# Decoder layer, attention stage: the split of the projected queries moves from ScalarE and VectorE (out of PSUM) to GpSimd (out of an SBUF copy), and the weight blocks stand in other pairs

## The chip, the cores and the metric

The kernel runs on one core of one Trainium2 chip. The metric is the device time of one execution, in microseconds (us). TensorE is called PE in the profile, VectorE DVE, ScalarE ACT, GpSimd POOL and SyncE SP; SP issues nearly all of the DMAs.

## The reference, cut to what matters

One decoder layer on four sequences of 512 tokens with 1024 features, in float32: a state-space mixer, then cross-attention over 1601 keys per sequence, then a feed-forward layer with 4-bit weights (3584 inner features), each followed by a residual add and a layer norm. The change is in the cross-attention, 16 heads with a latent of 64:

```python
C_q = Q @ Wq_d                                   # (b, n, 128)
C_kv = K @ Wkv_d                                 # (b, nkv, 64)
CqWqk = (C_q @ W_qk).reshape(b, n, H, LKV)       # the projection: queries of each head
scores = jnp.einsum('bnhl,bkl->bhnk', CqWqk, C_kv) / sqrt(LKV)
attn = softmax(scores)
out = jnp.einsum('bhnk,bkhd->bnhd', attn, (C_kv @ Wv_u).reshape(b, nkv, H, HD))
```

The weights of the feed-forward layer come as integers with integer zeros; `weight - zero` is formed for 84 blocks of 128 x 1024 while the attention runs.

## The kernel before, in words

Three stages run one after the other: the mixer (to about 318 us), the attention (to about 1426 us) and the feed-forward layer (to the end).

The attention handles four batches (sequences) of 16 heads, that is 64 heads; a head has four units of 128 queries, so there are 256 units (`NU`), numbered u or k, and 64 units to a batch. Two units make a pair (`PAIRS` = 128, 32 to a batch), numbered p. Heads are projected two at a time, so every eight units form one cycle with one projection.

Every engine walks the same loop over k, in an order written out by hand. In step k, PE computes the second half of the scores of unit k (L1019), then a projection (L999), an output product (L1057) or a turn of latent keys where one is due, then half of a weighting product (`weigh`, L1038), the transposes of the last three key tiles of unit k-1 (`turn`, L1048), and the first half of the scores of unit k+1. DVE takes the maximum of the second half of unit k (`maximum`, L1190), then what is due, then transposes the probabilities of unit k-1 in blocks (`turn`, L1197) into `tn`, then the maximum of the first half of unit k+1 (`first_maximum`, L1179). ACT computes the exponents of both halves (`exponent`, L1101), and PE may write the second half of the scores of unit k+1 only after the exponent of the second half of unit k has left that bank. ACT also copies the turned tiles (`keep_turned`, L1108), the weighted latents (`out_latent`, L1122) and, after each odd step, two of the blocks of a pair (`cross`, L1116).

The transposed blocks of a pair must change partitions before PE can weigh with them: SP moves nine of 16 blocks by DMA (`exchange`, L912), POOL copies five (`blocks`, L1315) and ACT two. Three buffers `pt` take them. The transposed tiles `tn` have two buffers, so DVE's transposes of pair p+2 wait until all blocks of pair p have moved (`moved`).

POOL's order in pair p: the five block copies; in odd pairs the sums of the denominators (L1322) and the residual add of a head (L1330); then, if the pair has a weight block, `prepare` (L1357 subtracts the zeros, L1359 casts); then steps of the layer norm of the batch before (`root_step` in pairs 17 to 19 of a batch, `factors` and `normalise`, L1334, in pairs 20 to 23); in pair 2 of two batches `split_keys` (L1305, L1307). SP's order in pair p: the store of the block of pair p-1, which waits for POOL's cast (L926); the exchange; the load of the next block; rows of the layer norm in pairs 23 to 30. `FREE` names the 11 of 32 pairs of a batch without a weight block; 84 blocks stand in the other pairs.

A score is computed with queries and keys each split in a high part (rounded to fp32r) and a low part (the rest). High and low parts of a query share the 128 partitions of `qs`: for the first head of a projection the high part stands in partitions 0 to 63 and the low part in 64 to 127, for the second head the other way round. Before the change, ACT writes the two high parts from the projection's PSUM bank `mi` (L1087, L1088), and DVE subtracts them from the same bank (L1172, L1174). This is done at steps k with k % 8 = 5, for the heads whose scores begin three units later. The bank `mi` is shared in a fixed order by projections, transposes, outputs and latent turns; after a projection the next one waits for DVE's second subtraction (`bank_free`, L897).

Of the kernel before, what the change touches and what calls it, by code (L numbers as in the profile page):

```python
# [11 lines left out]
P = 128  # L12
# [14 lines left out]
LAT = 64  # L27
# [760 lines left out]
PER_BATCH = len(BLOCKS) // L  # L788
FREE = (2, 5, 8, 11, 14, 20, 21, 22, 23, 30, 31)
LATE = 3 * (PAIRS // L)  # L790
# [32 lines left out]
def attention(nc, d, kvd, cq, ident, shared, raw, wint, x1, x2):  # L823

    with ExitStack() as ctx:
# [11 lines left out]
        s_cnp, s_cn = sem("cn_ps"), sem("cn")  # L837
        s_q, s_qh, s_ql = sem("q"), sem("qh"), sem("ql")
        s_sc, s_nm, s_ex, s_tt = (sem(n) for n in ("scores", "nm", "ex", "turned"))
# [9 lines left out]
        keys = keys_of(shared)  # L849
        wqk, wv, cn, kv = (keys[n] for n in ("wqk", "wv", "cn", "kv"))  # L850
        y0 = sb("b_y0", [P, QT, HID])
        rw = [sb(f"b_rw{j}", [P, HID], I32) for j in range(2)]
# [8 lines left out]
        pt.append(shared[:, NXC + 2 * NSZ - 8 * SEG:NXC + 2 * NSZ].rearrange("p (a z e) -> p a z e", a=4, z=2))  # L861
        pe = [sb(f"b_pe{j}", [P, NKT - NDT, 2, P]) for j in range(3)]
        ot = sb("b_ot", [P, NB])
        yo = sb("b_yo", [P, 2, QT, LAT])
# [28 lines left out]
        def bank_free(eng, ev):  # L893
            if AT[ev]:
                kind, g, e = EVENTS[AT[ev] - 1]
                if kind == "project":
                    eng.wait_ge(s_ql, g + 2)  # L897
                elif kind == "turn":
                    eng.wait_ge(s_pe, g + 1)
                elif kind == "cn":  # L900
                    eng.wait_ge(s_cn, 2 * (g - 1) + e + 1)
                else:
                    eng.wait_ge(s_yo, g + 1)
# [177 lines left out]
        def scalar():  # L1081
# [3 lines left out]
            def project(g):  # L1085
                S.wait_ge(s_q, g // 2 + 1)
                S.copy(qs[g // 2 % 2][0:LAT, 0, :], mi[0:LAT, :]).then_inc(s_qh, 1)  # L1087
                S.copy(qs[g // 2 % 2][LAT:P, 1, :], mi[LAT:P, :]).then_inc(s_qh, 1)  # L1088

# [62 lines left out]
        def vector():  # L1152
# [15 lines left out]

            def project(g):
                q = qs[g // 2 % 2]  # L1170
                V.wait_ge(s_qh, g + 1)
                V.tensor_tensor(q[LAT:P, 0, :], mi[0:LAT, :], q[0:LAT, 0, :].bitcast(F32), ALU.subtract).then_inc(s_ql, 1)  # L1172
                V.wait_ge(s_qh, g + 2)
                V.tensor_tensor(q[0:LAT, 1, :], mi[LAT:P, :], q[LAT:P, 1, :].bitcast(F32), ALU.subtract).then_inc(s_ql, 1)  # L1174
# [88 lines left out]
            low_keys(0)  # L1263
            project(0)
            low_keys(1)
# [4 lines left out]
            for k in range(NU + OUT_AT):  # L1270
                if k < NU:
                    maximum(k)
                if k % 8 == 5 and k + 3 < NU:
                    project((k + 3) // 4)
                if k % 4 == OUT_AT % 4 and k >= OUT_AT:
                    output((k - OUT_AT) // 4)
                if k in CN_AT:
                    keep_latent(*CN_AT[k])
                if 1 <= k <= NU:
                    turn(k - 1)  # L1280
                if k + 1 < NU:
                    first_maximum(k + 1)
                if k < NU:
                    norm_piece(k)
# [15 lines left out]
        def gpsimd():  # L1300
# [8 lines left out]
            def blocks(p):  # L1309
# [4 lines left out]
                for n, (a, c) in enumerate(BY_POOL):  # L1314
                    G.tensor_copy(pt[p % MOVES][32 * c:32 * c + 32, a, :, :], tn[s][32 * a:32 * a + 32, c, :, :]).then_inc(s_block, 1)  # L1315
                    G.wait_ge(s_block, len(BY_POOL) * p + n + 1)

            def sums(g):
# [44 lines left out]
            for p in range(PAIRS + 4):  # L1363
# [15 lines left out]
                if n == 2 and 1 <= b <= 2:  # L1379
                    split_keys(b + 1)  # L1380

        late, last_stores = sync()
# [582 lines left out]
```

## Time and profile before

| what | before |
|---|---|
| median of 3 runs | 2738.9 us (2735.4 to 2747.54) |
| the profiled execution | 2740.16 us, its span 2738.2 us |
| granted PE clock | 0.988 of full speed |
| busy over the span | PE 95%, DVE 85%, POOL 72%, ACT 61% |
| busy from 600 to 700 us (attention) | PE 96.60, DVE 92.52, POOL 79.25, ACT 77.03 us of 100 |

The span is the time from the first to the last instruction, and 2.0 us of the profiled execution lie around it. A matmul's end is modelled and overlaps the next matmul, so a busy PE says little; what counts is the distance from one score product to the next. "Idle before" tells how long an engine sat idle ahead of an instruction and which engine released it.

### The profile page before, as it was taken

What the parts mean: (1) busy time and instruction counts of PE and PEld (TensorE: products, weight loads), DVE (VectorE), ACT (ScalarE), POOL (GpSimd) and SP (SyncE); (2) the same over time, 40 slices, a digit from 0 to 9 for tenths busy, and PEclk for the clock granted to TensorE, in tenths of its full rate; (3) what the DMA queues carried; (4) which work ended last, traced back from release to release, by engine and by line L of the source; (5) the groups of instructions that cost most, each with busy time, mean ns of one, the idle gap of its engine ahead of it and who ended that gap; (6) DMA issues with size and microseconds to landing.
All of it is one profiled execution on the core that took longest, in us unless ns stands there. A gap on an engine that the chain in (4) does not pass through costs nothing.

```text
span 2738.2 us, 42011 instructions
## 1 busy us (share of the span) xinstructions
PE 2602.3 (95%) x14328; PEld 1979.5 (72%) x14328; DVE 2315.4 (85%) x2664; ACT 1670.2 (61%) x2619; POOL 1966.1 (72%) x1473
## 2 busy tenths in 40 slices
PE   7998899999999999999988999999999999999997
PEld 4665666666666666666656888888888888788885
DVE  2766688989998999899857999899998899899988
ACT  3444687877787778787855445454455555555553
POOL 1002377677777778777857999999887888888883
PEclk9899999999999999999999999999999999999999
DMA  7426677687778776877681222112223222132221
GB/s 276 157 100 206 212 236 216 188 240 206 223 214 261 206 219 204 259 228 221 201 278 69 100 93 93 70 70 70 77 70 123 77 85 78 70 116 79 83 93 77
DMA packets 166792, 420.64 MB, mean 154 GB/s; under 512 B 30130, under 2 KB 57652, under 8 KB 166068
## 3 DMA queue, kind: packets, MB, share of 16 engines
q1 hardware_dynamic: 164276, 409.57, 47.2%
q10 hardware_dynamic: 2304, 8.39, 0.8%
q8 instruction: 115, 1.88, 0.3%
q14 instruction: 97, 0.79, 0.1%
HBM read 248.43 MB, written 75.04 MB: 118 GB/s over the span
## 4 chain that ended last, share of the span: by engine, by line
PE 44%; SPq 3%; DVE 2%; POOL 1%; issue 1%; ACT 1%; DMA 1%; POOLq 0%; ACTq 0%; DVEq 0%
PE c_ps L1610 42%; SPq L912 2%; PE c_ps L1622 1%; DVE c_sum_g L1766 0%; DVE c_stats L1826 0%; DMA c_ident<-in_ident 0%; POOL b_rw L1357 0%; PE c_ps L1631 0%; POOL c_sum_g L1851 0%; PE b_po L1038 0%; PE b_sc L1019 0%; DVE c_acc L1766 0%; DMA b_rz<-in_c_dz 0%; DMA b_rz<-in_c_gz 0%; ACT c_sg L1674 0%
## 5 line engine op out<-in xcount | busy, mean ns | idle before, releaser
L1766 DVE SCALAR_TENSOR_TENSOR c_acc<-c_ps,c_sd,c_acc 128x1024 f32<-128x1024 f32 x440 | 562.9, 1282 | 90.8 <-PE c_ps L1610 90.7
L1668 ACT ACTIVATE c_scaled<-c_ps,c_sgu 128x1024 f32<-128x1024 f32 x336 | 375.2, 1117 | 422.5 <-PE c_ps L1610 414.7
L1101 ACT ACTIVATE b_pr<-b_sc,b_nm 128x799 f32<-128x799 f32 (+1 forms) x512 | 477.7, 935 | 169.4 <-DVE b_pr L1190 146.9
L1851 POOL TENSOR_TENSOR c_sum_u<-c_sum_u,c_scaled 128x1024 f32<-128x1024 f32 x168 | 404.8, 2410 | 99.6 <-ACT c_scaled L1668 98.3
L1851 POOL TENSOR_TENSOR c_sum_g<-c_sum_g,c_scaled 128x1024 f32<-128x1024 f32 x168 | 405.1, 2411 | 73.2 <-ACT c_scaled L1668 72.2
L1019 PE MATMUL b_sc<-b_kh,b_qs 128*128 128x402 f32 (+1 forms) x1024 | 398.6, 389 | 45.0 <-ACT b_pr L1101 41.2
L1197 DVE STREAM_TRANSPOSE b_tn<-b_pr 128x1280 f32<-128x1280 f32 x256 | 385.4, 1506 | 28.7 <-ACT b_pr L1101 14.6
L1315 POOL COPY b_pt<-b_tn 32x640 f32<-32x640 f32 x430 | 307.4, 715 | 141.7 <-DVE b_tn L1197 82.5
L1019 PE MATMUL b_sc<-b_kl,b_qs 128*128 128x402 f32 (+1 forms) x1024 | 355.9, 348 | 0.0
L1766 DVE SCALAR_TENSOR_TENSOR c_sum_g<-c_ps,c_sgu,c_sum_g 128x1024 f32<-128x1024 f32 x224 | 286.4, 1278 | 26.0 <-PE c_ps L1610 20.6
L1190 DVE TENSOR_SCALAR_CACHE_REDUCE b_pr<-b_sc,b_nm_first 128x799 f32<-128x799 f32 x256 | 268.7, 1050 | 29.1 <-PE b_sc L1019 8.3
L1766 DVE SCALAR_TENSOR_TENSOR c_sum_u<-c_ps,c_sgu,c_sum_u 128x1024 f32<-128x1024 f32 x224 | 285.7, 1276 | 6.5 <-POOL c_sum_u L1851 4.4
L1610 PE MATMUL c_ps<-c_hh,c_dw_int 128*128 128x512 f32 x896 | 277.9, 391 | 11.3 <-POOL c_hl L1867 7.1
L1179 DVE TENSOR_REDUCE b_nm_first<-b_sc 128x1 f32<-128x802 f32 x256 | 250.8, 980 | 44.8 <-PE b_sc L1019 40.3
L1610 PE MATMUL c_ps<-c_xh,c_gw_int 128*128 128x512 f32 x896 | 279.6, 393 | 5.3 <-DVE c_sum_u L1766 3.8
L1610 PE MATMUL c_ps<-c_xh,c_uw_int 128*128 128x512 f32 x896 | 278.6, 392 | 3.4 <-DVE c_xl L1771 2.3
L1019 PEld LDWEIGHTS b_sc<-b_kh,b_qs 128*128 128x128 f32 x1024 | 193.6, 189 | 119.0 <-ACT b_pr L1101 77.0
L1610 PE MATMUL c_ps<-c_xl,c_gw_int 128*128 128x512 f32 x896 | 277.0, 390 | 0.0
L1610 PE MATMUL c_ps<-c_hl,c_dw_int 128*128 128x512 f32 x896 | 276.6, 390 | 0.0
L1610 PE MATMUL c_ps<-c_xl,c_uw_int 128*128 128x512 f32 x896 | 276.5, 390 | 0.0
L1038 PE MATMUL b_po<-b_pt,shared 128*64 128x256 f32 x1720 | 258.9, 389 | 3.4 <-DMA b_pt<-b_tn 2.6
L764 POOL TENSOR_TENSOR a_xt<-a_xt,a_bup 128x1024 f32<-128x1024 f32 x16 | 37.6, 2355 | 264.6 <-DMA a_xt<-in_a_x 207.5
(212 smaller groups left out, 4871.0 us busy)
## 6 DMA issues: line engine op xcount, KB each, us to landing
b_pt<-b_tn SPq DMA_DIRECT2D x774, 80.0 KB, 2.7
shared<-b_tn SPq DMA_DIRECT2D x378, 80.0 KB, 2.8
c_uw_int<-wint_u SPq DMA_DIRECT2D x56, 512.0 KB, 3.5
c_gw_int<-wint_g SPq DMA_DIRECT2D x56, 512.0 KB, 3.4
c_dw_int<-wint_d SPq DMA_DIRECT2D x56, 512.0 KB, 3.4
a_cx<-in_b_ctxT SPq DMA_DIRECT2D x16, 1608.0 KB, 9.8
b_rw<-in_c_gw SPq DMA_DIRECT2D x28, 512.0 KB, 4.1
b_rz<-in_c_gz SPq DMA_DIRECT2D x28, 512.0 KB, 5.6
```

Source lines behind the costliest of these rows:

```text
L912: Q.dma_start(pt[p % MOVES][32 * c:32 * c + 32, a, :, :].rearrange("p t e -> p (t e)"), tn[s][32 * a:32 * a + 32, c, :, :].rearrange("p t ...
L1019: ins = T.matmul(sc[:, at:at + n], qs[g // 2 % 2][:, g % 2, q * P:(q + 1) * P], k[b % 2][:, k0:k0 + n], start=(z == 0), stop=(z == 1))
L1038: ins = T.matmul(po[z * LAT:(z + 1) * LAT, s * 256:(s + 1) * 256], cn[:, b, t, :], turned, start=(t < 2), stop=(t >= NKT - 2))
L1101: S.activation(pr[u % 2][:, k0:k1], sc[:, at + lo:at + hi], ACT.Exp, bias=nm[:, u % 2:u % 2 + 1], accum_out=den[:, g % 2, q, half:half + 1 ...
L1179: V.tensor_reduce(nm0[:, u % 2:u % 2 + 1], sc[:, at + SIDE[0][0]:at + SIDE[0][1]], AX, ALU.max, negate=True).then_inc(s_part, 1)
L1190: V.tensor_scalar(pr[u % 2][:, SIDE[1][2]:SIDE[1][3]], sc[:, at + SIDE[1][0]:at + SIDE[1][1]], -1.0, nm0[:, j], ALU.mult, ALU.min, accum_o ...
L1197: V.transpose(tn[u // 2 % 2][:, :, u % 2, :], pr[u % 2][:, 0:4 * SEG].rearrange("p (c e) -> p c e", c=4)).then_inc(s_tt, 1)
L1315: G.tensor_copy(pt[p % MOVES][32 * c:32 * c + 32, a, :, :], tn[s][32 * a:32 * a + 32, c, :, :]).then_inc(s_block, 1)
L1610: ins = T.matmul(pair[slot % 4][:, b * 512:(b + 1) * 512], w[n][t % 2][:, k * P:(k + 1) * P], v[:, b * 512:(b + 1) * 512], start=(z == 0), ...
L1668: S.activation(dst[:, :], pair[SLOT[x, t] % 4][:, :], ACT.Identity, scale=scale(x, t)).then_inc(s_e, 1)
L1766: V.scalar_tensor_tensor(out=total, in0=pair[SLOT[x, t] % 4][:, :], scalar=scale(x, t), in1=before, op0=ALU.mult, op1=ALU.add).then_inc(s_ ...
L1851: G.tensor_tensor(total, total, scaled[m % 2][:, :], ALU.add).then_inc(s_add, 1)
```

## The change

ACT now copies the whole projection bank (128 x 512) to a new SBUF tile `qf` in one instruction, and the bank is free after that copy. POOL makes the high parts and the low parts from `qf` in four instructions, at the end of its pairs p with p % 4 = 1; 31 projections go this way. The first projection (g = 0) keeps the old way. The pairs without a weight block become 1, 2, 5, 9, 13, 17, 21, 23, 25, 29 and 31 of each batch instead of 2, 5, 8, 11, 14, 20, 21, 22, 23, 30 and 31; their number stays at 11.

```diff
-FREE = (2, 5, 8, 11, 14, 20, 21, 22, 23, 30, 31)
+FREE = (1, 2, 5, 9, 13, 17, 21, 23, 25, 29, 31)
...
+        qf = shared[:, keys_end:keys_end + NB]
...
                 if kind == "project":
-                    eng.wait_ge(s_ql, g + 2)
+                    eng.wait_ge(s_qf, g // 2) if g else eng.wait_ge(s_ql, 2)
...
             def project(g):
                 S.wait_ge(s_q, g // 2 + 1)
-                S.copy(qs[g // 2 % 2][0:LAT, 0, :], mi[0:LAT, :]).then_inc(s_qh, 1)
-                S.copy(qs[g // 2 % 2][LAT:P, 1, :], mi[LAT:P, :]).then_inc(s_qh, 1)
+                if g == 0:
+                    S.copy(qs[0][0:LAT, 0, :], mi[0:LAT, :]).then_inc(s_qh, 1)
+                    S.copy(qs[0][LAT:P, 1, :], mi[LAT:P, :]).then_inc(s_qh, 1)
+                else:
+                    S.wait_ge(s_ql, g)
+                    S.copy(qf, mi[:, :]).then_inc(s_qf, 1)
...
-            def project(g):
-                q = qs[g // 2 % 2]
-                V.wait_ge(s_qh, g + 1)
+            def project_first():
+                q = qs[0]
+                V.wait_ge(s_qh, 1)
...
             for k in range(NU + OUT_AT):
                 if k < NU:
                     maximum(k)
-                if k % 8 == 5 and k + 3 < NU:
-                    project((k + 3) // 4)
...
+            def split_queries(g):
+                q = qs[g // 2 % 2]
+                G.wait_ge(s_qf, g // 2)
+                for z, (high, low) in enumerate(((slice(0, LAT), slice(LAT, P)), (slice(LAT, P), slice(0, LAT)))):
+                    G.tensor_copy(q[high, z, :], qf[high, :]).then_inc(s_qh, 1)
+                    G.wait_ge(s_qh, g + z + 1)
+                    G.tensor_tensor(q[low, z, :], qf[high, :], q[high, z, :].bitcast(F32), ALU.subtract).then_inc(s_ql, 1)
+                    G.wait_ge(s_ql, g + z + 1)
...
                 if n == 2 and 1 <= b <= 2:
                     split_keys(b + 1)
+                if p % 4 == 1 and 2 * p + 6 < NU:
+                    split_queries((p + 3) // 2)
```

## Rows read from the trace of the kernel before

**Rows 1.** PE timeline, score products: start us, us long, [idle before, releaser].

```profile
351.77 0.45 PE L1019 MATMUL b_sc<-b_kh,b_qs 128*128 128x402 f32 x1 [1.07 <-ACT b_pr L1101]
...
779.49 0.35 PE L1019 MATMUL b_sc<-b_kh,b_qs 128*128 128x402 f32 x1
...
783.73 0.43 PE L1019 MATMUL b_sc<-b_kh,b_qs 128*128 128x402 f32 x1
...
788.24 0.45 PE L1019 MATMUL b_sc<-b_kh,b_qs 128*128 128x402 f32 x1 [0.45 <-ACT b_pr L1101]
...
791.45 0.45 PE L1019 MATMUL b_sc<-b_kh,b_qs 128*128 128x402 f32 x1
...
792.54 0.43 PE L1019 MATMUL b_sc<-b_kh,b_qs 128*128 128x402 f32 x1
...
796.45 0.35 PE L1019 MATMUL b_sc<-b_kh,b_qs 128*128 128x402 f32 x1
...
1368.81 0.45 PE L1019 MATMUL b_sc<-b_kh,b_qs 128*128 128x402 f32 x1 [0.44 <-ACT b_pr L1101]
```

**Rows 2.** DVE timeline of the same cycle.

```profile
777.62 1.51 DVE L1197 STREAM_TRANSPOSE b_tn<-b_pr 128x1280 f32<-128x1280 f32 x1
...
780.79 1.05 DVE L1190 TENSOR_SCALAR_CACHE_REDUCE b_pr<-b_sc,b_nm_first 128x799 f32<-128x799 f32 x1
...
781.91 0.69 DVE L1172 TENSOR_TENSOR b_qs<-b_mi,b_qs 64x512 fp32r<-64x512 f32 x1
782.62 0.69 DVE L1174 TENSOR_TENSOR b_qs<-b_mi,b_qs 64x512 fp32r<-64x512 f32 x1
...
785.99 1.05 DVE L1190 TENSOR_SCALAR_CACHE_REDUCE b_pr<-b_sc,b_nm_first 128x799 f32<-128x799 f32 x1
```

**Rows 3.** ACT timeline of the same cycle.

```profile
781.29 0.58 ACT L1087 CAST b_qs<-b_mi 64x512 fp32r<-64x512 f32 x1 [0.94 <-PE b_mi L999]
...
785.31 1.47 ACT L1116 COPY shared<-b_tn 32x640 f32<-32x640 f32 x2
787.17 0.93 ACT L1101 ACTIVATE b_pr<-b_sc,b_nm 128x799 f32<-128x799 f32 x1 [0.39 <-PE b_mi L1048]
```

**Rows 4.** Who waited for whom, whole span: us in total, times, longest.

```profile
PE b_sc L1019 <- ACT b_pr L1101: 41.2, 83, 1.8
...
PE b_po L1038 <- DMA shared<-b_tn: 3.5, 3, 2.5
...
DVE b_tn L1197 <- DMA b_pt<-b_tn: 6.4, 4, 2.3
DVE b_tn L1197 <- DMA shared<-b_tn: 5.7, 3, 3.4
...
SPq L927 <- POOL b_rw L1359: 41.1, 41, 3.0
```

**Rows 5.** Groups by line, 480 to 1400 us: busy us, mean ns | idle before.

```profile
L1122 ACT COPY b_ot<-b_po 128x512 f32<-128x512 f32 x55 | 31.7, 576 | 0.0
...
L1334 POOL TENSOR_SCALAR b_y<-b_y,b_rstd,b_nmr 128x1024 f32<-128x1024 f32 x12 | 14.5, 1205 | 0.6
...
L1307 POOL TENSOR_TENSOR b_kl<-shared,b_kh 128x1601 fp32r<-128x1601 f32 x2 | 7.3, 3635 | 0.2
...
L1305 POOL CAST b_kh<-shared 128x1601 fp32r<-128x1601 f32 x2 | 3.0, 1521 | 0.1
```

**Rows 6.** POOL timeline of an odd pair with a weight block.

```profile
812.22 3.82 POOL L1315 COPY b_pt<-b_tn 32x640 f32<-32x640 f32 x5 [1.07 <-DVE b_tn L1197]
...
816.97 2.37 POOL L1357 TENSOR_TENSOR b_rw<-b_rw,b_rz 128x1024 int32<-128x1024 int32 x1
819.40 1.04 POOL L1359 CAST b_rw<-b_rw 128x1024 fp32r<-128x1024 int32 x1
```

**Rows 7.** Durations of one line: ns min/median/max, first and last start us.

```profile
L1315 POOL COPY b_pt<-b_tn x430: 707/714/726, 335.4 to 1415.1; 32x640 f32<-32x640 f32 x144
```

**Rows 8.** Page, part 1: each engine's busy us (share of the span) xinstructions.

```profile
PE 2602.3 (95%) x14328; PEld 1979.5 (72%) x14328; DVE 2315.4 (85%) x2664; ACT 1670.2 (61%) x2619; POOL 1966.1 (72%) x1473
```

More of the change, by code:

```diff
@@ L837, in attention @@
         s_cnp, s_cn = sem("cn_ps"), sem("cn")
-        s_q, s_qh, s_ql = sem("q"), sem("qh"), sem("ql")
+        s_q, s_qh, s_ql, s_qf = sem("q"), sem("qh"), sem("ql"), sem("q_kept")
         s_sc, s_nm, s_ex, s_tt = (sem(n) for n in ("scores", "nm", "ex", "turned"))
@@ L850, in attention @@
         wqk, wv, cn, kv = (keys[n] for n in ("wqk", "wv", "cn", "kv"))
+        keys_end = KPAD + 2 * HEADS * LAT + L * NKT * LAT
         y0 = sb("b_y0", [P, QT, HID])
@@ L1167, in keep_latent @@
                               mi[:, 0:len(chunk) * LAT].rearrange("p (t e) -> p t e", e=LAT)).then_inc(s_cn, 1)
-            def project(g):
-                q = qs[g // 2 % 2]
-                V.wait_ge(s_qh, g + 1)
+            def project_first():
+                q = qs[0]
+                V.wait_ge(s_qh, 1)
                 V.tensor_tensor(q[LAT:P, 0, :], mi[0:LAT, :], q[0:LAT, 0, :].bitcast(F32), ALU.subtract).then_inc(s_ql, 1)
-                V.wait_ge(s_qh, g + 2)
+                V.wait_ge(s_qh, 2)
                 V.tensor_tensor(q[0:LAT, 1, :], mi[LAT:P, :], q[LAT:P, 1, :].bitcast(F32), ALU.subtract).then_inc(s_ql, 1)
@@ L1263, in vector @@
             low_keys(0)
-            project(0)
+            project_first()
             low_keys(1)
```

## Prediction

> **What bounds the kernel now.** I read the PE timeline first, as starts of the second-half score product (L1019), one per unit. The rows at 779.49, 783.73, 788.24, 792.54 and 796.45 [rows 1] are units 109 to 113; 109 % 8 = 5, so the projection falls in the first step. The steps last 4.24, 4.51, 4.30 and 3.91 us. The reader is to see that three of the four carry no idle time: PE runs from product to product. Only the third start (788.24) waited, for ACT's exponent. The second and the fourth step hold the same PE work (scores, the first part of a weighting product, three transposes): 3.91 without a wait, 4.51 with it. So the stall costs 0.60 us. It is more than the 0.45 shown as idle, since the rows let one matmul's modelled end overlap the next. This start stands in each of the 31 cycles with a projection inside the loop, the first at 351.77 and the last at 1368.81, with 0.44 us of idle or more. Between these two lie 240 units, 30 cycles: 1017.04 / 30 = 33.90 us a cycle, 8.48 a pair.
>
> Then the DVE timeline of the same cycle [rows 2]. The maximum of unit 109 ends about 781.85; two subtractions follow from 781.91 to 783.31; only then comes the transpose and the next first-half maximum, and the maximum of unit 110 starts at 785.99. Its scores began at 783.73; for unit 109 the maximum began 780.79 - 779.49 = 1.30 after them, here 2.26. DVE is late by about 1 us because of the 1.4 us of subtractions. Last, ACT [rows 3]: it waits 0.94 for the projection, spends 1.2 on two copies, runs through a block copy from 785.31 to 786.78, and starts the exponent that PE waits for at 787.17, after 0.39 of waiting. The view names PE as the releaser there, but what came in just then is DVE's maximum (785.99 + 1.05 + 0.08 of read-out). So the split of the queries sets PE's stall, by way of DVE.
>
> The view of waits shows the rest [rows 4]: 41.2 us of PE idle for exponents in 83 waits, of which the 31 above are the largest regular part. Most of the others stand two steps ahead of the next projection, behind ACT's other block copies, and stay. DMA of moved blocks costs DVE 12.1 us in 7 waits and PE 3.5 in 3, near the ends of batches. SP waits for POOL's cast 41 times.
>
> **The change, part by part.** *DVE* loses 2 x 0.69 plus gaps, 1.4 us, 31 times [rows 2]. The transpose moves up to 781.9, and the first-half maximum of unit 110 is then ready when its scores are (they end a little before 783.73); the maximum of unit 110 can start about 1.1 to 1.3 after 783.73, at 785.0, not 785.99. *ACT* swaps two copies of 0.58 for one; the nearest row is its copy of a whole bank, 128x512 in 0.576 [rows 5], so it gains 0.6 us, and its block copy ends near 786.2. The exponent then starts at 786.2 to 786.3 and frees the bank near 787.2, while PE is ready only at 783.73 + 3.91 = 787.64. PE's own work covers all of it with 0.4 to spare: 31 x 0.60 = **18.6 us gained**. ACT's new wait on the split of the projection before is eight units old and costs nothing. The bank is released at 781.87 instead of 783.31; PE's transposes want it at about 783.5, so little is gained there. Steps where layer-norm statistics also sit on DVE start with DVE less late; I add 3 us for them (some ten steps at about 0.3), between bounds of 0 and 10 (the rest of the 41.2 that isn't ACT's).
>
> *POOL* gains four instructions, 31 times. The cast of 128x1601 took 1521 ns and the subtraction 3635 [rows 5], that is 0.95 and 2.27 ns an element; for 512 elements 0.49 and 1.16. Shorter instructions cost more an element: a block copy takes 714 ns for 640 [rows 7], 1.12 each, so 0.57 for 512, and by the same addition 1.25 for the subtraction. With a wait for its own result behind each, a split takes 2 x 1.82 and some gaps, 3.7 to 4.0; I take 3.9, in all 121 us on an engine that is busy for 1966.1 [rows 8]. Only half of the partitions are used; the block copies use 32 and take no less an element, so I expect no saving. No row has a subtraction that writes other partitions than it reads; block copies that do lie in the same 707 to 726 ns, so I take none as the extra, and keep 7 us a split as the far end.
>
> What hides it: an odd pair with a block takes from 812.22 to 820.44, 8.2 us [rows 6]; an even one lacks sums and residual add (816.04 to 816.97), 7.3; an odd pair without a block and with a split 4.75 + 3.9 = 8.65. The new order gives, in four pairs, 7.3 + 8.65 + 7.3 + 8.2 = 31.45 against a cycle of 33.3 (33.9 less 0.6). POOL fits, with 1.85 us to spare. The split's deadline: the transpose that releases the pair ends at 779.13 [rows 2], the scores that need the first head start at 791.45 [rows 1]: 12.3 us, 11.7 after the gain. POOL needs 4.75 for the pair's own work and 1.95 for the first head: 6.7. It may be 5 us late before PE waits.
>
> It is late once in each batch but the first. Pairs 17 to 22 now hold splits in 17 and 21, blocks in 18, 19, 20 and 22, and a root step or a normalise (1.2 us, [rows 5]; the root steps I cost alike) in each: 8.65 + 7.3 + 8.2 + 7.3 + 8.65 + 7.3 + 6 x 1.2 = 54.6 against 6 x 8.3 = 49.8. POOL ends 4.8 us late, where pairs 20 to 23 were free of blocks before. Late next is SP: it issues the store of a pair's block ahead of the next exchange, and the nine block moves, the next load and the norm's rows queue behind that wait. The cast of pair 22 comes 4.8 + 7.3 = 12.1 after its transposes, so exchange 23 starts some 4 us late. In the trace such waits reached 3.0 us and 41.1 in all, with only 7 DVE waits on moves [rows 4], so I charge 1.5 us in three batches: **4.5 lost**, between 0 and 5 us a batch.
>
> *The weight blocks.* Before, runs of five and six pairs with blocks stood one after the other in each batch (15 to 19, 24 to 29); now none is longer than three. The 15.6 us of waits for moved blocks [rows 4] came behind the long runs near batch ends. I let 9 of them go, between 0 and 15.6.
>
> **Sum.** 18.6 + 3 + 9 - 4.5 = 26 us off the profiled execution's 2740.2 (span 2738.2 and 2.0 around it): 2714. The profiled execution is 1.3 us above the median of 2738.9; the forecast stays at **2714**, 0.9% below the median.
>
> **Rivals.** (a) *POOL and SP eat the gain.* The lateness in pairs 17 to 23 isn't absorbed: about 5 us a batch in three batches, and the waits at batch ends stay: 18.6 + 3 - 15 = 7 off, 2733. For it: POOL's load rises by 121 us and the store wait couples it to SP. Against: POOL is idle again by pair 31.
>
> (b) *Slower: the split takes longer.* The place is POOL in pairs 1, 5, 9 and so on. From 3.9 + 1.85 = 5.75 us a split on, POOL sets the cycle; beyond 6.4 the cycle exceeds 33.9; at 7 it is 34.55, 0.65 x 31 = 20 us slower: 2760. For it: the shifted, two-input form has no row.
>
> (e) *Slower: the splits block DVE.* Before, DVE gave 1.4 us a cycle; held off for the 3.9 of a split it would lose 2.5 x 31 = 78 us: up to 2818; it decides from 1.4 us of blocking a split on. The block copies keep to 707 to 726 ns beside a DVE that is busy for nine tenths [rows 7], so nothing that the two do now blocks. The Trainium skill, Perfetto Trace Analysis, Optimizing Scalar/DVE Operations, warns that VectorE and GpSimd share an SBUF read port, so that moving work between them might not help; by that rule (e) would come true, and the trace doesn't agree so far.
>
> (c) *All moved-block waits go and the layer-norm pairs cost nothing*: 18.6 + 3 + 15.6 = 37 off, 2703.
>
> (d) *PE's stall stays*, because ACT's block copy alone holds back the exponent. Then only 9 - 4.5 = 4.5 are left: 2736. Against: the 0.39 that ACT idled ahead of that exponent [rows 3], and the 0.6 it gains.
>
> **Chances and range.** Forecast 0.55 (its own range 2706 to 2722), (a) 0.15, (b) 0.07, (e) 0.03, (c) 0.12, (d) 0.08. The measurement tells about 0.5%, 14 us. Forecast and (c) are faster, and a third of (a): 0.72; the rest of (a) and (d), within 0.5%: 0.18; (b) and (e), slower: 0.10. The range takes in (a), (c) and (d) with their bounds and leaves out (b) and (e): 2698 to 2741.
>
> **What the new profile would show.** Right: no start of a score product behind k % 8 = 6 waits for ACT, the second step is 3.9 instead of 4.5, the cycle near 33.2; ACT's bank copy takes 0.58; POOL's cast and subtraction on 64x512 take 0.5 to 0.6 and 1.15 to 1.3. Waits of DVE for moved blocks shrink near pairs 28 to 31 and appear at 23 to 25. The forecast is wrong if PE waits for POOL's split, if DVE's transposes or POOL's copies get longer, or if the exponent of step 6 stays as late as before.

## The result, and the profile after

The changed kernel takes 2727.1 us in the median of 5 runs (2725.0 to 2727.4), against 2738.9: ratio 0.9948, 95% interval 0.9932 to 0.9963. The profiled execution takes 2725.14 us with a span of 2721.3, that is 15.0 us less than before, where the sum of the prediction said 26 less (2714). The range (2698 to 2741) and the sign hold; the sum is 11 us too good, and the forecast's own range (2706 to 2722) is missed by 5. Lines have moved: scores L1019 is L1021, DVE's maximum L1190 is L1196, its transposes L1197 are L1203, ACT's exponent L1101 is L1107, the weighting product L1038 is L1040, SP's moves L912 and store L927 are L914 and L929, GpSimd's subtraction and cast of a weight block L1357 and L1359 are L1370 and L1372; new are ACT's bank copy L1094 and the split, L1326 and L1328.

The PE timeline of the kernel after: second-half score products of units 13, 101 to 105, and 253, which answer to [rows 1].

```profile
373.62 0.35 PE L1021 MATMUL b_sc<-b_kh,b_qs 128*128 128x402 f32 x1
...
736.32 0.35 PE L1021 MATMUL b_sc<-b_kh,b_qs 128*128 128x402 f32 x1
...
740.55 0.43 PE L1021 MATMUL b_sc<-b_kh,b_qs 128*128 128x402 f32 x1
...
744.46 0.35 PE L1021 MATMUL b_sc<-b_kh,b_qs 128*128 128x402 f32 x1
...
748.67 0.43 PE L1021 MATMUL b_sc<-b_kh,b_qs 128*128 128x402 f32 x1
...
752.58 0.35 PE L1021 MATMUL b_sc<-b_kh,b_qs 128*128 128x402 f32 x1
...
1379.39 0.35 PE L1021 MATMUL b_sc<-b_kh,b_qs 128*128 128x402 f32 x1
```

The steps from 736.32 are 4.23, 3.91, 4.21 and 3.91, and no start waits. Before they were 4.24, 4.51, 4.30 and 3.91. The undisturbed cycle of eight units fell from 33.03 to 32.33 us: 0.60 at the stalled step, as forecast, and 0.1 at the next.

DVE's timeline of this cycle, which answers to [rows 2], and below it ACT's, which answers to [rows 3].

```profile
737.61 1.05 DVE L1196 TENSOR_SCALAR_CACHE_REDUCE b_pr<-b_sc,b_nm_first 128x799 f32<-128x799 f32 x1
...
738.59 1.51 DVE L1203 STREAM_TRANSPOSE b_tn<-b_pr 128x1280 f32<-128x1280 f32 x1
740.50 0.99 DVE L1185 TENSOR_REDUCE b_nm_first<-b_sc 128x1 f32<-128x802 f32 x1 [0.40 <-PE b_sc L1021]
741.60 1.05 DVE L1196 TENSOR_SCALAR_CACHE_REDUCE b_pr<-b_sc,b_nm_first 128x799 f32<-128x799 f32 x1
```

```profile
738.12 0.59 ACT L1094 COPY shared<-b_mi 128x512 f32<-128x512 f32 x1 [0.94 <-PE b_mi L1001]
...
741.60 1.47 ACT L1122 COPY b_pt<-b_tn 32x640 f32<-32x640 f32 x2
743.09 0.93 ACT L1107 ACTIVATE b_pr<-b_sc,b_nm 128x799 f32<-128x799 f32 x1
```

The transpose follows the maximum at once, and the next maximum starts 1.05 us behind its scores (741.60 against 740.55) where it was 2.26. The exponent at 743.09 starts straight behind ACT's block copy: DVE's maximum was in at 742.65, so ACT is now the last in that step, with little to spare.

GpSimd's lines and ACT's copy after: ns min/median/max, first and last start (the block copies answer to [rows 7]).

```profile
L1326 POOL CAST b_qs<-shared x62: 599/607/613, 345.9 to 1352.9; 64x512 fp32r<-64x512 f32 x62
```

```profile
L1328 POOL TENSOR_TENSOR b_qs<-shared,b_qs x62: 1257/1277/1292, 346.5 to 1353.6; 64x512 fp32r<-64x512 f32 x62
```

```profile
L1319 POOL COPY b_pt<-b_tn x430: 706/713/723, 334.5 to 1399.0; 32x640 f32<-32x640 f32 x144
```

```profile
L1094 ACT COPY shared<-b_mi x31: 585/586/587, 343.4 to 1348.5; 128x512 f32<-128x512 f32 x31
```

So far all is as costed: 0.61 and 1.28 where 0.57 and 1.25 were taken, a split lasts 4.0 us with its gaps, for 3.9, and block copies are as long as before. The page, part 1, which answers to [rows 8], has GpSimd 112 us busier and DVE 41 us less:

```profile
PE 2598.3 (95%) x14328; PEld 1982.2 (73%) x14328; DVE 2274.3 (84%) x2602; ACT 1651.3 (61%) x2588; POOL 2078.3 (76%) x1597
```

The loss is in the waits. Waits of the whole span after, which answer to [rows 4]:

```profile
PE b_sc L1021 <- ACT b_pr L1107: 29.7, 59, 1.6
...
DVE b_tn L1203 <- DMA b_pt<-b_tn: 12.3, 10, 2.5
...
DVE b_tn L1203 <- DMA shared<-b_tn: 7.3, 5, 2.7
DVE b_tn L1203 <- issue: 7.2, 5, 4.1
...
PE b_po L1040 <- DMA shared<-b_tn: 5.0, 3, 2.3
```

SP's own waits, 340 to 1430 us:

```profile
SPq L929 <- POOL b_rw L1372: 53.6, 41, 4.5
```

PE waits 29.7 us for exponents, not 41.2. But the three rows of waits for moved blocks that [rows 4] has (12.1 on DVE, 3.5 on PE) now sum to 24.6, not 15.6, and SP stands 53.6 us before GpSimd's casts, not 41.1. The row "issue" (0.5 us before) is more of the same: in each of its five cases a move had landed 0.08 us ahead of the transpose. The prediction let 9 of the 15.6 go.

The stretch from unit 13 to unit 253 (30 cycles) splits the result in two: 30 undisturbed cycles, and the rest, which is what late blocks, statistics and the like add.

| | 13 to 253 | 30 undisturbed cycles | rest |
|---|---|---|---|
| before | 1018.5 | 30 x 33.03 = 990.9 | 27.6 |
| after | 1005.8 | 30 x 32.33 = 969.9 | 35.9 |
| change | -12.7 | -21.0 | +8.3 |

The prediction had -18.6 in the first column of changes and -7.5 (3 and 9 off, 4.5 on) in the second. The first came out 2.4 better; the second missed by 15.8. (Of the span's 16.9 us, 1.6 are gained ahead of unit 13 and 2.6 behind unit 253.) How one such late step arises is seen in the longest, that of unit 112: it lasts from 781.42 to 789.43, 8.0 us, and 3.91 undisturbed. SP's timeline ahead of it:

```profile
769.46 0.58 SPq L921 DMA_DIRECT2D b_rw<-in_c_gw  x1
770.09 0.43 SPq L924 DMA_DIRECT2D b_rz<-in_c_gz  x1
770.62 1.12 SPq L947 DMA_DIRECT2D shared<-kvd  x2
771.78 0.58 SPq L929 DMA_DIRECT2D wint_d<-b_rw  x1
772.47 5.66 SPq L914 DMA_DIRECT2D shared<-b_tn  x9
```

GpSimd's, of the same time, and PE's:

```profile
771.24 1.21 POOL L1347 TENSOR_SCALAR b_y<-b_y,b_rstd,b_nmr 128x1024 f32<-128x1024 f32 x1
...
777.16 1.21 POOL L1347 TENSOR_SCALAR b_y<-b_y,b_rstd,b_nmr 128x1024 f32<-128x1024 f32 x1
778.31 0.61 POOL L1326 CAST b_qs<-shared 64x512 fp32r<-64x512 f32 x1
...
781.03 1.28 POOL L1328 TENSOR_TENSOR b_qs<-shared,b_qs 64x512 fp32r<-64x512 f32 x1
782.38 3.81 POOL L1319 COPY b_pt<-b_tn 32x640 f32<-32x640 f32 x5
```

```profile
784.65 2.38 PE L1040 MATMUL b_po<-shared 128*64 128x256 f32 x14 [2.25 <-DMA shared<-b_tn]
```

The nine moves are those of pair 21 of its batch. Pair 20 had no weight block before; now two loads of rows and the store of pair 20's block go out ahead of them, beside the next batch's keys, which stood there before, too. They were issued by 778.13, and PE gets what they bring at 784.65, 6.5 us later. GpSimd is late too: with two normalise steps and a split behind it, it begins the copies of pair 22 at 782.38, 6.0 us after that pair's last transpose (774.91 + 1.50). The new order alone is enough for such a step: in free_only, the kernel before with only that order (next section), the steps of units 112 and 113 are together 4.2 us longer than undisturbed ones.

The step cost PE more than its wait: PE sat idle for 2.25 us, and the step is 4.1 us too long. Most of the rest goes with TensorE's granted clock, seen in these two windows (us; busy us and instructions of PE, PEld, DVE, ACT and POOL; granted clock; DMA share; GB/s):

```profile
784.00:785.00 1.00, 0.34 (x4) 0.28 (x6) 0.31 (x1) 0.00 (x0) 0.94 (x2) 1.00 0.61 159
787.00:788.00 1.00, 1.00 (x5) 1.00 (x5) 0.89 (x2) 0.00 (x0) 1.00 (x1) 0.50 1.02 418
```

Behind the wait the granted clock is 0.50, that is 1.2 of 2.4 GHz, from 786 to 789 us, and score products last 0.54 us, for 0.35. Between 340 and 1390 us the trace of after has two such stretches (the other lies from 1346 to 1349), that of before has one.

### The profile page after: what moved, and what is told of

Read it like the earlier page. It is cut to its first block, busy times and chain, and to the rows that moved or that the text cites. A ratio compares the mean times of both kernels' runs of the same rounds, so it can differ in the third digit from the quotient of the medians.

```text
span 2721.3 us, 42088 instructions
## 1 busy us (share of the span) xinstructions
PE 2598.3 (95%) x14328; PEld 1982.2 (73%) x14328; DVE 2274.3 (84%) x2602; ACT 1651.3 (61%) x2588; POOL 2078.3 (76%) x1597
## 4 chain that ended last, share of the span: by engine, by line
PE 48%; POOL 5%; SPq 4%; ACT 2%; DVE 2%; issue 2%; DMA 1%; POOLq 0%; ACTq 0%; DVEq 0%
PE c_ps L1625 43%; SPq L914 3%; PE b_po L1040 2%; PE b_sc L1021 2%; POOL b_pt L1319 1%; POOL b_rw L1370 1%; PE c_ps L1637 1%; POOL shared L1319 1%; ACT b_pr L1107 1%; PE b_mi L1050 0%; POOL b_rw L1372 0%; DVE c_sum_g L1781 0%; POOL b_qs L1328 0%; DVE c_stats L1841 0%; POOL c_sum_g L1866 0%
## 5 line engine op out<-in xcount | busy, mean ns | idle before, releaser
L1107 ACT ACTIVATE b_pr<-b_sc,b_nm 128x799 f32<-128x799 f32 (+1 forms) x512 | 477.1, 933 | 176.5 <-DVE b_pr L1196 158.1
L1021 PE MATMUL b_sc<-b_kh,b_qs 128*128 128x402 f32 (+1 forms) x1024 | 397.1, 388 | 35.9 <-ACT b_pr L1107 29.7
L1203 DVE STREAM_TRANSPOSE b_tn<-b_pr 128x1280 f32<-128x1280 f32 x256 | 385.4, 1506 | 39.0 <-DMA b_pt<-b_tn 12.3
L1021 PE MATMUL b_sc<-b_kl,b_qs 128*128 128x402 f32 (+1 forms) x1024 | 356.1, 348 | 0.0
L1196 DVE TENSOR_SCALAR_CACHE_REDUCE b_pr<-b_sc,b_nm_first 128x799 f32<-128x799 f32 x256 | 268.6, 1049 | 30.0 <-PE b_sc L1021 9.4
L1021 PEld LDWEIGHTS b_sc<-b_kh,b_qs 128*128 128x128 f32 x1024 | 193.7, 189 | 103.2 <-ACT b_pr L1107 58.4
L1040 PE MATMUL b_po<-b_pt,shared 128*64 128x256 f32 x1720 | 258.9, 389 | 1.8 <-DMA b_pt<-b_tn 1.0
```

The source lines that it names most:

```text
L1021: ins = T.matmul(sc[:, at:at + n], qs[g // 2 % 2][:, g % 2, q * P:(q + 1) * P], k[b % 2][:, k0:k0 + n], start=(z == 0), stop=(z == 1))
L1040: ins = T.matmul(po[z * LAT:(z + 1) * LAT, s * 256:(s + 1) * 256], cn[:, b, t, :], turned, start=(t < 2), stop=(t >= NKT - 2))
L1107: S.activation(pr[u % 2][:, k0:k1], sc[:, at + lo:at + hi], ACT.Exp, bias=nm[:, u % 2:u % 2 + 1], accum_out=den[:, g % 2, q, half:half + 1 ...
L1196: V.tensor_scalar(pr[u % 2][:, SIDE[1][2]:SIDE[1][3]], sc[:, at + SIDE[1][0]:at + SIDE[1][1]], -1.0, nm0[:, j], ALU.mult, ALU.min, accum_o ...
L1203: V.transpose(tn[u // 2 % 2][:, :, u % 2, :], pr[u % 2][:, 0:4 * SEG].rearrange("p (c e) -> p c e", c=4)).then_inc(s_tt, 1)
```

## The experiments

Each line below is one kernel; "rest" is the distance from unit 13 to unit 253 less 30 of its own undisturbed cycles, from its profiled execution alone, and the two sums of waits are those of 340 to 1430 us (rows named "issue" left out). The experiments were timed beside runs of before with medians of 2741.6 to 2742.9, so the ratios compare better than the medians do. Executions of one kernel differ by up to 13 us (old_free: 2738.3 to 2751.4), and the profiled one of store_mid is 5.8 us below its median, so a difference of a few us in the rest says little where the ratios don't tell two kernels apart.

| kernel | median us | ratio to before, interval | cycle | rest | SP waits for casts | DVE and PE wait for moves and GpSimd's copies |
|---|---|---|---|---|---|---|
| before | 2738.9 | | 33.03 | 27.6 | 41.1 | 19.5 |
| after | 2727.1 | 0.9948, 0.9932 to 0.9963 | 32.33 | 35.9 | 53.6 | 31.0 |
| free_only | 2730.7 | 0.9968, 0.9956 to 0.9980 | 33.03 | 21.6 | 20.1 | 14.7 |
| old_free | 2743.8 | 1.0011, 0.9999 to 1.0023 | 32.33 | 51.3 | 69.8 | 37.1 |
| dve_filler | 2729.4 | 0.9961, 0.9949 to 0.9972 | 32.68 | 26.6 | 43.1 | 28.1 |
| act_two | 2728.6 | 0.9962, 0.9947 to 0.9976 | 32.68 | 32.1 | 59.1 | 32.2 |
| split_double | 2766.2 | 1.0092, 1.0075 to 1.0109 | 32.33 | 78.8 | 127.0 | 63.2 |
| norm_short | 2720.5 | 0.9931, 0.9914 to 0.9948 | 32.33 | 31.8 | 43.4 | 28.7 |
| order20 | 2724.4 | 0.9949, 0.9931 to 0.9968 | 32.33 | 35.6 | 52.3 | 27.0 |
| store_late | 2738.8 | 0.9992, 0.9982 to 1.0003 | 32.33 | 48.8 | none shown | 50.1 |
| prep_short | 2711.3 | 0.9878, 0.9863 to 0.9894 | 32.33 | 20.4 | 0.4 | 19.2 |
| rz_short | 2720.0 | 0.9914, 0.9900 to 0.9928 | 32.33 | 27.7 | 61.0 | 23.1 |
| prep_first | 2722.3 | 0.9929, 0.9917 to 0.9941 | 32.33 | 36.1 | 45.7 | 29.7 |
| store_mid | 2719.4 | 0.9908, 0.9893 to 0.9924 | 32.33 | 27.2 | 6.8 | 25.4 |

**The two parts alone.** free_only is the kernel before with only the new order of the weight blocks; old_free is the kernel after with the old order.

```diff
-FREE = (2, 5, 8, 11, 14, 20, 21, 22, 23, 30, 31)
+FREE = (1, 2, 5, 9, 13, 17, 21, 23, 25, 29, 31)
```

> The kernel before with only the new order of the weight blocks; the queries are split by ScalarE and VectorE as before. Theory (VectorE's subtractions make TensorE's stall, the order does not): the start of the score product behind k % 8 = 6 still waits 0.44 us or more in all 31 cycles, the cycle stays near 33.0, and the time lies within 10 us of 2739, since the order only moves the waits for moved blocks. Rival (the order of the blocks makes the gain): about 2727.

> The changed kernel with the old order of the weight blocks, so that GpSimd's splits fall on pairs that have a block too (1, 9, 13, 17, 25, 29 of a batch). Theory: plain cycles keep 3.91 us in the step k % 8 = 6, but such a pair costs GpSimd 8.2 + 3.9 = 12.1 us against a pair of 8.2, so it is 4 us late there, more in the long runs 15 to 19 and 24 to 29, TensorE waits for the split or the moved blocks, and the time is 5 to 40 us above 2727. Rival (the order is neutral, GpSimd has slack enough): 2727.

In free_only the stall is unchanged, as this start of its PE timeline shows, and the rest falls by 6.0. The time, 2730.7, lies in the theory's window, but at its edge: the order has a gain of its own.

```profile
749.48 0.46 PE L1019 MATMUL b_sc<-b_kh,b_qs 128*128 128x402 f32 x1 [0.45 <-ACT b_pr L1101]
```

In old_free the stall is gone and the cycle is 32.33, but the rest grows by 23.7 and eats all of it. Its waits:

```profile
DVE b_tn L1203 <- DMA b_pt<-b_tn: 19.8, 11, 2.5
...
DVE b_tn L1203 <- DMA shared<-b_tn: 10.7, 6, 3.0
...
PE b_sc L1021 <- POOL b_qs L1328: 8.5, 6, 2.1
```

So the order alone is worth 0.3%, the split alone nothing, and both together 0.5%. They don't add: the order pays for part of what the split costs GpSimd.

**What the stall was.** dve_filler puts a maximum over 1280 columns of an SBUF tile on DVE (1.48 us, its result unused) where the two subtractions stood.

```diff
+                if k % 8 == 5 and k + 3 < NU:
+                    V.tensor_reduce(idle[:, :], shared[:, KPAD:KPAD + 1280], AX, ALU.max)
```

> The changed kernel, with an unused maximum over 1280 columns (about 1.4 us) on VectorE where the two subtractions stood, 31 times; it reads SBUF and nothing waits for it. Theory: TensorE's stall at k % 8 = 6 comes back with 0.4 to 0.6 us in the 31 cycles, 14 to 19 us: 2741 to 2746. Rival (ScalarE's single copy or the early release of the bank removed the stall): 2727 to 2730.

DVE's timeline of dve_filler in the cycle of unit 101:

```profile
741.23 1.05 DVE L1197 TENSOR_SCALAR_CACHE_REDUCE b_pr<-b_sc,b_nm_first 128x799 f32<-128x799 f32 x1
...
742.20 1.48 DVE L1281 TENSOR_REDUCE b_idle<-shared 128x1 f32<-128x1280 f32 x1
...
746.09 1.05 DVE L1197 TENSOR_SCALAR_CACHE_REDUCE b_pr<-b_sc,b_nm_first 128x799 f32<-128x799 f32 x1
```

From maximum to maximum DVE needs 4.86 us here, 5.20 before (780.79 to 785.99, [rows 2]) and 3.99 after; the step is 4.18, 4.51 and 3.91. From 5.20 to 4.86 both fall by about a third of a microsecond. The filler holds DVE for less time than the subtractions did (the transpose behind it starts 2.37 us after the maximum, for 2.56), and it brings back only 0.27 of the 0.60. The exponent that PE waits for is late because of DVE here, as ACT's timeline shows:

```profile
747.26 0.93 ACT L1108 ACTIVATE b_pr<-b_sc,b_nm 128x799 f32<-128x799 f32 x1 [0.58 <-DVE b_pr L1197]
```

That DVE's lateness makes the stall stands; the size that was expected of the filler doesn't, and the time, 2729.4, lies in the rival's window. The new fact is in the total: 30 cycles are 0.35 longer, 10.5 us, and the kernel is slower by only 2 (by the ratios some 4, and their intervals overlap), because the rest shrinks by 9.3.

act_two copies the bank in two halves on ACT, 0.59 us more in a cycle.

```diff
-                    S.copy(qf, mi[:, :]).then_inc(s_qf, 1)
+                    for half in (slice(0, LAT), slice(LAT, P)):
+                        S.copy(qf[half, :], mi[half, :]).then_inc(s_qf, 1)
```

> The changed kernel with the bank copied in two halves of 64 partitions, so that ScalarE spends 1.2 us as before the change and the bank is released 0.6 us later. Theory: TensorE's own work covers it (0.4 us to spare in my working), the time rises by 0 to 6 us over 2727. Rival (ScalarE's saved 0.6 us is what removed the stall): the stall at k % 8 = 6 comes back, 2741 to 2746.

The step becomes 4.15, so of the 0.59 added 0.24 shows, and ACT had 0.35 to spare, for the 0.4 of the prediction. ACT's side, too, was thus worth part of the stall: with its two copies left, only 0.36 of the 0.60 would have gone. Here the rest falls by only 3.8 of the 10.5 us that 30 cycles are longer: the stretch from unit 13 to unit 253 is 6.7 us longer than after. The profiled time hides it (2727.1, for 2725.1), because this execution was 4.4 us shorter ahead of unit 13, and the ratio isn't told apart from that of the kernel after.

**How much GpSimd can take.** split_double does each subtraction of a split twice, which makes a split some 6.6 us, for 4.0.

```diff
+                    G.tensor_tensor(q[low, z, :], qf[high, :], q[high, z, :].bitcast(F32), ALU.subtract).then_inc(s_qh, 1)
+                    G.wait_ge(s_qh, 2 * (g + z))
```

> The kernel after, with each of the two subtractions of a split done twice on GpSimd: 2 x 1.28 us and two waits more, 2.6 to 2.8 us in each of 31 cycles. Theory (GpSimd has 32.3 - 31.5 = under 1 us of a cycle to spare, so from there on it sets the cycle): cycles grow by 1.7 to 2.2 us, 50 to 65 us in all, 2775 to 2795. Rival (GpSimd is late only in places and has the time elsewhere, as its share of busy time of 0.76 says): 2730 to 2745.

It is slower than after by 39.1 us, 1.26 in each of 31 cycles, for 2.6 to 2.7 more work: GpSimd had about 1.4 us of a cycle to spare, and neither figure expected fits. In the waits the excess stands where it was looked for: SP waits 127 us for casts, DVE and PE 63 for moves. The prediction's rival (b) would have come true with such a split, and more sharply than it said: it put the point from which the kernel is slower than before at 6.4 us a split, and one of 6.6 is 0.9% slower already, some 25 us.

**Where GpSimd's lateness comes from.** norm_short and order20 aim at pairs 17 to 25.

```diff
-                G.tensor_scalar(y[b % 2][:, q, :], y[b % 2][:, q, :], rstd[:, q:q + 1], nmr[:, q:q + 1],
+                G.tensor_scalar(y[b % 2][:, q, 0:4], y[b % 2][:, q, 0:4], rstd[:, q:q + 1], nmr[:, q:q + 1],
```

```diff
-FREE = (1, 2, 5, 9, 13, 17, 21, 23, 25, 29, 31)
+FREE = (1, 2, 5, 9, 13, 17, 20, 21, 25, 29, 31)
```

> The kernel after, with GpSimd's normalise of batches 0 to 2 done on 4 of 1024 columns (the rest of these rows is left without the layer norm): 12 instructions of 1.2 us shrink to about 0.1, in pairs 20 to 23 of batches 1 to 3. Theory (GpSimd's lateness of 5 to 7 us in pairs 20 to 24 makes the exchanges late and gives back part of the gain there): lateness at pair 22 falls to 2 to 3 us, the long steps of pairs 20 to 25 go, and the time falls by 4 to 9 us to 2718 to 2723. Rival (the lost time sits at the batch ends, pairs 27 to 31 and 0, with SP's row loads): under 2 us, 2725 to 2728.

> The kernel after, with pair 20 of each batch free of a weight block in place of pair 23; the split, ScalarE's copy and all else are the same. By GpSimd's own work (split pairs 8.65, even pairs with a block 7.3, odd ones 8.2, 1.2 more in pairs 17 to 23, against 8.08 a pair) it is then at most 3 us late in pairs 17 to 25, where it was up to 6.8 late. Theory (this lateness gives back part of the gain): 4 to 8 us faster than the kernel after, 2719 to 2723. Rival (the waits at the batch ends are what counts): 2725 to 2729.

norm_short's median lies in its window (2720.5, rest 4.1 less), but its interval overlaps that of the kernel after, so the gain isn't clear of the noise. GpSimd's start on pair 22 is 3.9 to 4.2 us late where it was 5.5 to 6.8; 2 to 3 had been expected. order20 misses its window: in its timeline pair 22 is 2.5 late, but pair 24 is 4.6, where it was 0.1 to 4.2. The lateness is moved, not worked off, and the time is that of the kernel after within its interval.

**SP's order.** SP issues the store of a block, which waits for GpSimd's cast, ahead of the next pair's nine moves. store_late issues it behind all nine, store_mid behind the fourth.

```diff
-                if p and block_of(p - 1) is not None:
-                    store(block_of(p - 1))
                 exchange(p)
+                if p and block_of(p - 1) is not None:
+                    store(block_of(p - 1))
```

```diff
-                for a, c in BY_DMA:
+                for m, (a, c) in enumerate(BY_DMA):
+                    if m == 4 and p and block_of(p - 1) is not None:
+                        store(block_of(p - 1))
```

> The kernel after, with one change on SP: the store of the pair before is issued behind the exchange of the pair, not ahead of it, so the wait for GpSimd's cast no longer stands in front of the block moves. Theory (part of TensorE's gain is given back because GpSimd is late, SP waits for its cast with the store, and the exchange behind it comes late): the waits of DVE and PE for moved blocks shrink from some 20 us to under 10, and the time falls to 2712 to 2720. Rival 1 (the moves are late for another reason, the transfers themselves or the load's wait for the last store): the same time, 2725 to 2729. Rival 2 (the store now comes later, so the loads of the rows do, and GpSimd waits for them): slower than 2730.

> The kernel after, with SP's store of the block before issued behind the fourth of the nine moves: the exchange starts without a wait, and GpSimd may be about 2.5 us later before SP waits; but the load of the next rows, two issues behind the moves, waits for this store to land, which takes 5 to 7 us, and only five moves (3.1 us) lie between. Theory (a store that is issued later holds up the loads, as when it stood behind the whole exchange): half of that loss, 2729 to 2735. Rival (the start of the moves is what counts): 2718 to 2724.

store_late lost the whole gain. The theory of that run (only the store's wait matters) fell, and its second rival is what the waits of store_late show:

```profile
SPq L921 <- DMA wint_g<-b_rw: 56.1, 20, 5.1
SPq L921 <- DMA wint_u<-b_rw: 53.2, 20, 4.2
```

```profile
POOL b_rw L1370 <- DMA b_rz<-in_c_dz: 33.2, 13, 4.6
```

The load of the next rows reuses the buffer of the block just stored, so it must wait for the store to land. After the moves, that wait has nothing to hide behind: SP stands 109 us in these two rows, the loads come late, and GpSimd waits for them (33.2, where after has 15.4). store_mid was expected to lose half as much, and this was wrong: it is the fastest version that computes the whole reference, 2719.4. SP's waits in store_mid:

```profile
SPq L923 <- DMA wint_u<-b_rw: 13.2, 17, 2.2
SPq L923 <- DMA wint_g<-b_rw: 7.3, 6, 3.0
SPq L931 <- POOL b_rw L1372: 6.8, 6, 2.4
```

Four moves ahead of the store hide 46.8 of the 53.6 us of waiting for the cast; the five behind it hide most of its landing. GpSimd itself is as late as in the kernel after (6.2 to 6.6 us on pair 22): its lateness cost time mainly by way of SP's wait.

**The two halves of the loop.** prep_short takes away GpSimd's conversion of the weights, rz_short most bytes of one of the two loads (so both leave most of the weights wrong), prep_first only changes GpSimd's order.

```diff
-                G.tensor_tensor(rw[i % 2][:, :], rw[i % 2][:, :], rz[i % 2][:, :], ALU.subtract).then_inc(s_sub, 1)
+                G.tensor_tensor(rw[i % 2][:, 0:64], rw[i % 2][:, 0:64], rz[i % 2][:, 0:64], ALU.subtract).then_inc(s_sub, 1)
...
-                G.tensor_copy(rw[i % 2][:, :].bitcast(F32R), rw[i % 2][:, :]).then_inc(s_cast, 1)
+                G.tensor_copy(rw[i % 2][:, 0:64].bitcast(F32R), rw[i % 2][:, 0:64]).then_inc(s_cast, 1)
```

```diff
+                w = HID if i < 2 else 64
...
-                Q.dma_start(rz[i % 2][:, :], raw[n + "z"][j:j + 1, :].broadcast_to([P, HID])).then_inc(s_rin[i % 2], 16)
+                Q.dma_start(rz[i % 2][:, 0:w], raw[n + "z"][j:j + 1, 0:w].broadcast_to([P, w])).then_inc(s_rin[i % 2], 16)
```

```diff
+                if p < PAIRS and block_of(p) is not None:
+                    prepare(block_of(p))
                 if p % 2 and p < PAIRS:
                     sums(p // 2)
                 if p % 2 and p >= 5:
                     output((p - 5) // 2)
-                if p < PAIRS and block_of(p) is not None:
-                    prepare(block_of(p))
```

> The kernel after, with GpSimd's subtraction and cast of a weight block done on 64 of 1024 columns (the weights stay unconverted): 85 times about 3.4 us of GpSimd shrink to about 0.4; all transfers stay. Theory 1 (GpSimd's work, made late by the splits, holds back SP's store and so the exchange): SP no longer waits for a cast, DVE's and PE's waits for moved blocks nearly go, and the time falls to 2707 to 2714. Theory 2 (the transfers hold the chain: the loads of the rows land late and the nine moves take SP 6.5 us of a pair's 8.1): the waits for moves stay at half or more, 2718 to 2727.

> The kernel after, with the second load of each weight block (the row of zero points, broadcast to 128 partitions, 512 KB) cut to 64 of 1024 columns behind the first two blocks; the number of DMA issues and all work of the engines stay. About a fifth of the bytes of a pair with a block go. Theory 2 (loads that land late make GpSimd late, 27.7 us in 21 waits, and its cast and the store then hold SP): GpSimd's waits for the zero points go, 2712 to 2720. Theory 1 (GpSimd's own work is what is late): 2724 to 2728.

> The kernel after, with GpSimd's work of a pair in another order: the weight block is converted ahead of the sums and the residual add of an odd pair, not behind them, so that the cast comes about 0.9 us earlier in odd pairs. Theory 1 (GpSimd's lateness holds the store): 1 to 4 us faster, 2723 to 2726. Rival (the sums come 3.4 us later and ACT and DVE wait for them): 2730 to 2740.

prep_short lands in the window of theory 1: with GpSimd always in time, SP's wait for casts is gone and the rest is 20.4. But DVE's and PE's waits for moves, which that theory expected to nearly go, stay at 19.2 of 31.0, as theory 2 had it. SP's wait in prep_short:

```profile
SPq L929 <- POOL b_rw L1372: 0.4, 2, 0.2
```

rz_short lands on the edge of theory 2's window. SP still waits 61 us for casts there, but GpSimd's waits for rows of zero points fall from 27.7 to 7.1 us, those of DVE and PE for moves from 31.0 to 23.1, and the rest is 8.2 less. Neither theory is the only one: conversion and transfers are two halves of one loop. prep_first is faster by 5 us in the median, but its interval overlaps that of the kernel after and its rest is no smaller, so it tells nothing for sure.

## Why the prediction was right, and where its sum failed

*The stall (18.6 us).* Right in mechanism and size. DVE's subtractions made the exponent of the second step late; without them that step is 3.91 in 23 of 31 cycles and at most 4.08 in five more (the other three, of units 6, 126 and 190, last 5.19 to 6.79, and lasted 5.14 to 6.72 before), and putting work back on DVE or ACT brings part of the stall back. The 0.1 gained at the next step was not forecast.

*ACT's 0.4 to spare.* Right: 0.35. Rival (d), that ACT alone keeps the stall, is refuted, and dve_filler shows that DVE did hold it.

*The split at 3.9 us.* Right: 4.0 (778.31 to 782.31). One sign of being wrong shows, though small: PE waits for the split 3 times, 2.4 us in all. Rival (e) needs block copies or transposes that get longer; the copies take 713 ns for 714, and DVE's transposes have a median of 1506 and a longest of 1515 ns in both traces. The rule in the Trainium skill, Perfetto Trace Analysis, Optimizing Scalar/DVE Operations, that work moved between these two engines might not help because of a shared port, is not borne out by these rows. In the Trainium skill it is a DVE operation on two ports that locks the other engine out, and no run here shows whether any of DVE's forms is one.

*The statistics (3 us).* Not found at that size: the steps with layer-norm work on DVE sum to 5.1 us over undisturbed ones before, and to 4.1 in prep_short, where few waits are left.

*The moved blocks: 9 off, and 4.5 on for GpSimd's lateness.* This is the step that failed. The 9 was read from the kernel before, whose GpSimd had no splits and whose cycle was 33.03. free_only has just that, and there the term is nearly right: the rest falls by 6.0. With the splits and a cycle shorter by 0.7, the rest then rises from 21.6 to 35.9, by 14.3, where 4.5 was charged. Sorted by the pair that a step weighs (the step of unit k has half of pair (k - 6) / 2), the time of the steps over undisturbed ones shows both terms:

| us over undisturbed steps | before | free_only | after | store_mid | prep_short |
|---|---|---|---|---|---|
| pairs 20 to 25 | 0 | 3.6 | 12.5 | 3.1 | 1.9 |
| pairs 26 to 31 | 14.1 | 5.0 | 8.7 | 11.0 | 7.0 |
| six steps with a turn of latent keys | 6.3 | 6.3 | 6.3 | 6.3 | 6.3 |

Near the batch ends 5.4 went where 9 were let go; in pairs 20 to 25 some 12.5 came on where 4.5 was charged. The place was right (GpSimd 5.5 to 6.8 us late on pair 22, the scores that wait for the split stand there, late moves after it), but the charge was three times too small, and the 9 and the 4.5 are not separate: both are the balance of one loop.

The loop is this. SP can't issue the moves before the store ahead of them, the store waits for GpSimd's cast, the cast waits for the loads of its rows, and the loads stand behind the moves before them on SP. Each link was cut or stretched in a run: no conversion (prep_short) takes 15.5 from the rest, a load with fewer bytes (rz_short) 8.2, a store that lets four moves go first (store_mid) 8.7; more work in GpSimd (split_double) adds 42.9, and a store that holds up the loads (store_late) 12.9. The loop has a pace of its own, and it had less to spare than the 1.85 us of a cycle that GpSimd's work alone left in the prediction. One reason is in the sum: it set 31.45 against 33.3, a mean cycle with its waits in it, where the undisturbed cycle is 32.33. The other, that GpSimd also waits for loads and SP for GpSimd, fits the runs but has no number of its own. dve_filler and act_two show it from the other side: PE's cycle longer by 0.35 lets the rest shrink by 9.3 and 3.8. So rival (a), that GpSimd and SP eat the gain, was half true, at 11 us instead of 19. That the range held is partly its width: it took in rivals (a), (c) and (d), any gain from 0 to 40 us.

In pairs 28 and 29 of batches 1 to 3 (counted from 0), SP starts its moves 2 to 6 us late in prep_short and store_mid, too. In batch 1 of prep_short SP's own issues fill its time there. SP's timeline, the moves of pairs 27 to 29:

```profile
819.47 7.92 SPq L914 DMA_DIRECT2D shared<-b_tn  x9
...
829.84 7.28 SPq L914 DMA_DIRECT2D b_pt<-b_tn  x9
...
839.72 6.04 SPq L914 DMA_DIRECT2D b_pt<-b_tn  x9
```

From 819.47 to 839.72 are 20.3 us for two pairs, 18.7 of them issues (behind each nine moves two loads of rows, a load for the layer norm and a store), where two undisturbed pairs last 16.2 (half of 32.33). What stays open: why nine moves take SP 7 to 8 us there and 5.6 at the least elsewhere, and how much of the rest of 20.4 beyond the 6.3 of the latent keys is the transfers' own.

## What to carry to other kernels

When the bound engine gets faster, look at queues that run beside it at its pace: here 8 of 21 us went to SP and GpSimd, which were late already in places and lost the time in which they caught up. Cost such a pair of in-order queues as one loop, with the waits of both in it, and not each engine by its busy time; GpSimd, busy for 76% of the span and for 88% of 340 to 1390 us, had only 1.4 us of a 32-us cycle free. Where one wait in a queue stands ahead of transfers that don't need it, moving it a few issues back can be worth more than any work saved (store_mid, 8 us); moved too far it meets the next wait.

## What the runs showed of the hardware that was not expected

The landing of small transfers depends on what was put into the queue before them. DMA issues of the kernel after, 700 to 1000 us: size, and median us from issue to landing.

```profile
b_pt<-b_tn SPq DMA_DIRECT2D x216, 80.0 KB, 2.7
...
wint_d<-b_rw SPq DMA_DIRECT2D x8, 512.0 KB, 7.0
```

The nine moves issued from 772.47 to 778.13, in the window 769.4 to 778.2 us:

```profile
shared<-b_tn SPq DMA_DIRECT2D x9, 80.0 KB, 7.1
```

A move lands 2.7 us after its issue in the median, but these took 7.1, where 1024 KB of rows, 800 KB of keys and a store of 512 KB had been issued just before (the step of unit 112 above). With the nine moves that is 3056 KB between 769.46 and 784.65, some 206 GB/s (a KB is 1024 bytes), near the 226 GB/s that the same stretch of 700 to 1000 us moves on average; this fits moves that land when all that stands ahead of them has gone. The Trainium skill, DMA: Bandwidth & Descriptors, Queues, rings and completion order, says that one DMA engine takes the descriptors of a ring in their order; this trace agrees, as far as it shows.

GpSimd's subtraction that reads 64 partitions and writes the other 64 took 1.277 us for 512 columns, 2.49 ns a column, where the subtraction on 1601 columns took 2.27 ([rows 5]). The cast, which stays in its partitions, rose as much, from 0.95 to 1.19 ns a column (0.607 us): crossing partitions cost nothing that shows.
